# A language-model tower, 32 sequences in 38 written-out steps: one product and six small pieces of work change places

## The reference

```python
combined = concatenate([pos_emb, nest_table[nesting], seg_table[segments]])   # embedding
h = combined @ W
x = layernorm(h)
q, k, v = split(x @ qkv_w.T + qkv_b)                    # 8 heads of 16
h = h + (softmax(q @ k.T / 4) @ v) @ out_w.T + out_b
x = layernorm(h)
adapted = softmax(x @ gate_w.T) - sigmoid(x @ thr_w.T) / 4      # 4 experts
w = relu(adapted); w = w / where(sum(w) == 0, 1, sum(w))
out = h + sum_e w[e] * (relu(x @ fc1_w[e].T) @ lora_A[e] @ lora_B[e] @ fc2_w[e].T)
```

## Time and profile before

| | us |
|---|---|
| median of 3 runs | 1270.54 |
| lowest, highest | 1269.72, 1273.03 |
| the profiled execution | 1269.83 |
| its span, first to last instruction | 1267.8 |
| mean granted clock of TensorE | 0.969 |
| TensorE busy | 1148.3 (91%) |
| VectorE busy | 933.7 (74%) |
| ScalarE busy | 809.8 (64%) |
| GpSimd busy | 591.9 (47%) |

### The profile page before, as it was taken

One profiled execution on the slowest core, in us unless ns is written; L12 is line 12 of the kernel. 1 busy time (PEld: TensorE's weight loads), 2 busy tenths in 40 slices (PEclk: granted clock), 3 DMA queues, 4 the chain that ended last, 5 costly groups with the idle time before them and its releaser, 6 DMA issues.

```text
span 1267.8 us, 25321 instructions
## 1 busy us (share of the span) xinstructions
PE 1148.3 (91%) x6328; PEld 467.2 (37%) x6328; DVE 933.7 (74%) x2401; ACT 809.8 (64%) x1570; POOL 591.9 (47%) x588
## 2 busy tenths in 40 slices
PE   3379899999999999999989999899999999999975
PEld 1123334344433343444334434333343344333323
DVE  6388777788878877787777788778868887778312
ACT  1127677766667777667767776667667667676741
POOL 1534554544555445345554444455535445542221
PEclk9679999999999999999999999999999999999986
DMA  2445443445445444354542454455443454541110
GB/s 79 98 112 106 95 107 97 100 104 110 106 118 113 103 98 96 94 114 108 120 113 79 104 104 105 101 119 119 101 99 82 103 116 103 116 116 42 42 56 30
DMA packets 88425, 124.51 MB, mean 98 GB/s; under 512 B 17469, under 2 KB 69054, under 8 KB 82054
## 3 DMA queue, kind: packets, MB, share of 16 engines
q1 hardware_dynamic: 79040, 114.00, 39.2%
q10 hardware_dynamic: 9230, 8.66, 3.0%
HBM read 80.80 MB, written 34.95 MB: 91 GB/s over the span
## 4 chain that ended last, share of the span: by engine, by line
PE 69%; DVE 11%; issue 6%; DMA 3%; POOL 1%; ACT 1%; DVEq 0%; POOLq 0%; SPq 0%; ACTq 0%
PE pv L632 16%; PE mix L642 15%; PE sc L621 14%; PE mix L690 8%; PE mix L659 4%; DVE bn L854 4%; PE mix L705 3%; DVE negmax L864 2%; PE mix L664 2%; PE mix L654 2%; PE mix L684 2%; PE mix L677 2%; DVE low L938 2%; DVE h_sb L849 1%; DMA den_dram<-ctx_sb 1%
## 5 line engine op out<-in xcount | busy, mean ns | idle before, releaser
L864 DVE TENSOR_REDUCE negmax<-mix 128x1 f32<-128x512 f32 x1024 | 678.5, 682 | 189.5 <-PE mix L642 188.8
L490 ACT ACTIVATE probs<-sc 128x512 f32<-128x512 f32 x1024 | 591.9, 600 | 295.1 <-PE sc L621 280.2
L621 PE MATMUL sc<-qstk,kstk 120*128 120x512 bf16 x1024 | 383.7, 383 | 3.6 <-DMA qstk<-mT 2.2
L642 PE MATMUL mix<-kstk,qstk 96*128 96x512 bf16 x1024 | 355.0, 389 | 23.9 <-issue 8.9
L443 POOL TENSOR_TENSOR ctxh<-ctx_sb,rdenb 128x512 f32<-128x512 f32 x64 | 81.2, 1270 | 430.5 <-DMA rdenb<-rden_dram 430.1
L632 PE MATMUL pv<-probs,vals 128*32 128x512 f32 x2048 | 273.3, 606 | 0.0
L642 PEld LDWEIGHTS mix<-kstk,qstk 96*128 96x128 bf16 x1024 | 100.1, 98 | 338.2 <-DVE negmax L864 156.7
L621 PEld LDWEIGHTS sc<-qstk,kstk 120*128 120x128 bf16 x1024 | 101.8, 100 | 126.1 <-ACT probs L490 55.8
L690 PE MATMUL mix<-xn2T,fc1T_sb 128*128 128x512 f32 x256 | 135.7, 615 | 1.2 <-ACT wT L555 1.0
L410 POOL TENSOR_TENSOR pieces<-qk,pieces 128x512 bf16<-128x512 f32 x64 | 73.9, 1155 | 38.6 <-ACT pieces L505 38.6
L560 ACT ACTIVATE hid<-mix 128x512 f32<-128x512 f32 x128 | 76.6, 598 | 18.4 <-PE mix L690 16.6
(11 more groups left out here) (113 smaller groups left out, 1078.1 us busy)
## 6 DMA issues: line engine op xcount, KB each, us to landing
stack_dram<-pieces SPq DMA_DIRECT2D x192, 128.0 KB
rdenb<-rden_dram SPq DMA_DIRECT2D x64, 256.0 KB
qstk<-stack_dram SPq DMA_DIRECT2D x32, 384.0 KB, 5.3
kstk<-stack_dram SPq DMA_DIRECT2D x32, 384.0 KB, 7.4
qstk<-stack_dram SPq DMA_DIRECT2D x32, 256.0 KB, 5.8
kstk<-stack_dram SPq DMA_DIRECT2D x32, 256.0 KB, 8.2
wrow<-w_dram SPq DMA_DIRECT2D x32, 256.0 KB
out<-out_sb SPq DMA_DIRECT2D x32, 256.0 KB, 4.5
```

Of the source, the lines that this page charges most:

```text
L490: act.activation(probs[:, c % 8, i % 2], sc[:, i % RING], ACT.Exp).then_inc(s_exp, 1)
L621: pe.matmul(sc[:, i % RING, :], kstk[0:KROWS, u, h, j * P:(j + 1) * P], qstk[0:KROWS, u, h, :], start=True, stop=True).then_inc(s_score, 1)
L642: pe.matmul(max_bank(m), qstk[0:STK, u, h, j * P:(j + 1) * P], kstk[0:STK, u, h, :], start=True, stop=True).then_inc(s_mxmm, 1)
L864: dve.tensor_reduce(negmax[:, m // NT, m % NT:m % NT + 1], max_bank(m), AX.X, ALU.max, negate=True).then_inc(s_max, 1)
```

## The change

Three things change together. `steps` writes out all 38 steps, with no loop, so that every wait is for a constant. In `PRODUCTS` the v product moves from slot 4 to slot 3 and the output product from slot 3 to slot 4, which swaps the banks they use; `finish` on VectorE moves with the output product, and v's copy on ScalarE with v. The reciprocals of the denominators stand at slot 6 ahead of the gate arithmetic, whose parts each move back by one or two places; `den_out` stands one place earlier and `gate_exp` one slot later. No instruction of arithmetic is added or removed.

```diff
 PRODUCTS = [
-    ("project", -2), ("embed", 3), ("low", -3), ("out", -3), ("v", 2), ("xn2T", -2), ("gates", -2), ("fc1_0", -2),
+    ("project", -2), ("embed", 3), ("low", -3), ("v", 2), ("out", -3), ("xn2T", -2), ("gates", -2), ("fc1_0", -2),
...
 ACT_WORK = [
-    (4, 0, "ctx", -1, 1), (4, 1, "v", 2, 0), (4, 2, "den_out", -1, 1), (5, 1, "xn2T", -2, 0), (6, 2, "gate_exp", -2, 0),
+    (3, 1, "v", 2, 0), (4, 0, "ctx", -1, 1), (4, 1, "den_out", -1, 1), (5, 1, "xn2T", -2, 0), (7, 1, "gate_exp", -2, 0),
...
 DVE_WORK = [
-    (3, 1, "finish", -3, 0), (6, 1, "gate", -2, 0),
-    (7, 0, "gate", -2, 1), (7, 1, "invert_den", -1, 0), (7, 2, "gate", -2, 2), (9, 0, "gate", -2, 3),
+    (4, 1, "finish", -3, 0), (6, 1, "invert_den", -1, 0), (6, 2, "gate", -2, 0), (7, 2, "gate", -2, 1),
+    (8, 2, "gate", -2, 2), (9, 1, "gate", -2, 3),
...
         def steps(eng, step):
-            first = 4
-            rounds = (NSEQ - 3 - first) // U
-            for t in range(-3, first):
-                step(t, t % U)
-            with eng.Fori(0, rounds) as i:
-                for u in range(U):
-                    step(i * U + (first + u), (first + u) % U)
-            for t in range(first + rounds * U, NSEQ + 3):
+            for t in range(-3, NSEQ + 3):
                 step(t, t % U)
```

## The result

| | before | changed |
|---|---|---|
| median, us | 1271.51 | 1329.87 |
| lowest, highest | 1269.72, 1273.03 | 1311.69, 1339.62 |
| ratio to before, 95% interval | | 1.036 (1.0325 to 1.0396) |
| profiled execution, span | 1269.83, 1267.8 | 1339.62, 1337.8 |

I had forecast 1241 us, faster with a chance of 0.92. The times go with the mean granted clock of TensorE: 0.955 at 1311.69 us, 0.945 at 1323.08, 0.941 at 1336.66 and 0.933 at 1339.62.

What follows compares the result with a forecast made beforehand. TensorE, busy 91% of the span, was taken as the bound, with pauses inside steps and at loop turns to remove. 1269.8 - 14.1 - 14.6 + 0.5 + 1.5 - 2.5 = 1240.6 us, 1241 as a median; 8-in-10 range 1230 to 1257.

Steps and rivals of the forecast that it cites:

- The loop: At the loop's five turns: writing the steps out removes all the extra time, 14.1 us (bounds 0 and 14.1).
- v ahead of the output product: Slot 3: TensorE waits less by 0.56 us in each of 26 steps, 14.6 us (bounds 0 and 27).
- The reciprocals ahead of the gates: Slot 6, VectorE waiting for denominators: costs 0.5 us over 26 steps and 1.5 us in attention's first two steps.
- the limit: Latest start of the reciprocals, 632.95, without stopping TensorE at slot 7's second maximum; each later microsecond costs one.
- (a): Slot 3: the pause only moves along VectorE's list, so 14.6 us are missing, 1255 us; chance 0.14.
- (d): Straight code pauses too: none of the 14.1 us gained, 1255 us, above 1270 at 1.2 us per step; chance 0.07.
- (b): Denominators come behind the output store (median 4.5 us): 0.9 us per step, 23 us, 1264 us; chance 0.11.
- Slower than before: Whole kernel: outcome slower than the kernel before, chance 0.05, as 0.03 from (c) and 0.02 from (d).
- (c): Denominators' store falls into the stacks' loads: reciprocals 2.35 us past the limit, 61 us, 1302 us; chance 0.03.
- The end: Last steps: last passes over the values and last denominators come earlier, saving 2.5 us (1 to 3).

Runs made afterwards that it cites:

- e1: Kernel before with only the 38 steps written out, its three tables unchanged: 1257.46 us, ratio 0.9888.
- e2: Kernel before, loop kept, with only v ahead of the output product and its copy and `finish` moved along: 1257.19 us, ratio 0.9894.
- e4: Kernel before with steps written out and v ahead of the output product, reciprocals and gates as before: 1238.68 us, ratio 0.9739.
- e5: Changed kernel plus one wait: GpSimd's `normalise` products start only after VectorE's four cutting operations on the row maxima: 1243.03 us, ratio 0.9766.
- e10: e4 plus three GpSimd additions of 128x512 per step that nobody reads, started with the last row maximum: 1306.38 us, ratio 1.027.
- e8: Changed kernel with the gate parts and the gates' exponential back at their old places, reciprocals still early: 1298.85 us, ratio 1.0218.

## Why the prediction was wrong

- **The loop, 14.1 us: right.** e1 gives 1272.1 - 1257.46 = 14.6 us.
- **v ahead of the output product, 14.6 us: right.** e2 gives 14.9 us, and v waits 0.51 us in its steady step (0.5 forecast).
- **Both: right.** e4 gives 33.4 us, with 28.7 forecast for the two. A part of the end's 2.5 us may be in it. A part is in the steps: without the loop they are 35.77 us (e1) and with v ahead 35.11, so 0.66 us each and not 0.56.
- **The reciprocals ahead of the gates, +0.5 and +1.5 us: this is the step that failed.** The part put down for it was a wait for the denominators, and that part came out better than forecast. SyncE issues their load 2.0 us behind their store, not 3.6, and the reciprocals start without a wait 14.50 us behind the projection in nearly all steady steps, where the prediction has 14.6 to 15.4 and the limit is 632.95 - 617.38 = 15.57. With the collision taken out the whole change measures 1243.03 us (e5), 2 us from the forecast of 1241. Even so this third part brings nothing: e5 is 4 us slower than e4, for the 0.24 us per step of the later gate parts, for which the sum had no term. In the second step of attention TensorE waits 2.87 us for VectorE, where it was 2.33 (changed kernel, timeline of TensorE):

```profile
132.59 0.39 PE L635 MATMUL mix<-kstk,qstk 96*128 96x512 bf16 x1 [2.87 <-DVE negmax L857]
```

What it left out is what the earlier reciprocals set off. Their new place was worked out on the lists of VectorE, ScalarE, SyncE and TensorE, and GpSimd's `normalise`, two steps down the chain, was not asked for its new time; the sum put its effect at nothing without a reason.
- **What stood in its place.** VectorE's small operations waited under GpSimd's products, up to 1.3 us each, and the row maximum behind them came late. In a steady step that is a wait of 2.26 us ahead of the q product and about 1.6 us more, 39.25 - 35.35 (e5) = 3.9 us together. The lower clock is most of that rest: by itself it cost 1.5 to 1.6 us in e10. For a new wait the prediction's rivals had no term for the clock. The kernel before showed it: the window with a pause at a loop turn has a clock of 0.95.
- **The rivals.** (a) and (d) did not happen: no new wait in slot 4 or 5, and no pause for issue in straight code. (b) did not happen in the changed kernel: the output store, issued later, lands in 2.3 us there, where its median was 4.5. That comes with the move of the output product, for the median is 4.3 in e1 and 2.4 in e2 (the last two columns are KB and median us to landing):

```profile
out<-out_sb SPq DMA_DIRECT2D x32, 256.0 KB, 2.3
```

- **Slower than before** had 0.05, from (c) and a part of (d). The place of (c), slot 7, and its cause, late denominators, were others, and the pauses of (d) did not come. None of the four was the mechanism, so the 0.05 had the wrong reason.
- **The end, 2.5 us:** not measured alone.

The rows to see it by were there: the operations of tile mpc ended 1.3 us before GpSimd's products began, and VectorE's one-hot comparison was long, 745 ns in the mean with 340 at the shortest, where it ran beside GpSimd's work. The duration of an instruction form that is large for its size is a question, and I did not ask it.

## What to carry to other kernels

When a piece is moved earlier, follow its consequences along the chain to the engines that it wakes, and lay their new times beside everything that runs there, even where no semaphore connects them. VectorE's operations with two SBUF inputs, or casts between SBUF tiles, should not lie under GpSimd's long instructions if TensorE waits for what comes behind them; a wait that holds GpSimd back for 2 us in each step was worth 69 us here (1312 at the least without it, 1243 with it). Make changes of a table one at a time: two of these three were worth 33 us, and the third hid them.

## What the runs showed of the hardware

- A VectorE operation of 0.17 to 0.2 us (two SBUF inputs, or a cast between SBUF tiles) that begins under a GpSimd addition or product of 128x512 in SBUF takes up to 1.3 us. In the changed kernel, e8 and e10 the slowed ones nearly all end within 0.07 us of the end of a GpSimd instruction, and VectorE's PSUM reductions beside it are unchanged (683 against 682 ns in the mean).
- A wait of TensorE of about 2.3 us was followed by a stretch at the lower of its two clock levels (mean granted clock 0.57 over 4 us) in the step shown. It did not follow every wait: 20 of 24 in the changed kernel, 7 of 25 in e8 and 7 of 27 in e10, where it cost 1.5 to 1.6 us each time.
- A turn of the hardware loop cost 2.8 to 2.9 us of the span in the mean (14.6 us for five), and the 24 steps of the loop, written out, cost nothing that the waits show.
